# Opening reordered around the first x load, and expert pairs normalised two pairs ahead

## The chip, the cores and the metric

The kernel runs on one NeuronCore of a Trainium2 chip. The metric is the device time of one execution in microseconds (us). The median of several executions is compared; a profiled execution has a time of its own.

## The reference

Input x has 64 sequences of 128 tokens, 256 wide (8192 tokens); ctx has 128 tokens of width 192 for each sequence. Two layers follow each other:

```python
# 1. gated cross attention, 16 heads of 16
q = layernorm(x) @ wq + bq;  k = ctx @ wk + bk;  v = ctx @ wv + bv
out = softmax(q @ k.T / 4) @ v
x = x + tanh(g_xattn) * (out @ wo + bo)
# 2. gated switch layer: 32 experts of hidden width 64, one expert for each token
h = layernorm(x)
e = argmax(h @ router_w.T + router_b)
y = relu(relu(h @ w1[e] + b1[e]) @ w2[e] + b2[e])
x = x + tanh(g_ffn) * y
```

## The kernel before, in words

Each engine has a program of its own, written out in full, and they meet only by semaphores: SP issues DMAs, POOL (GpSimd), ACT (ScalarE), DVE (VectorE) and PE (TensorE) work in the order of their program and stop at the first wait that is not met. Matrix products keep float32 accuracy by splitting each operand into a float16 "hi" part (a cast on ACT) and a "lo" part (a subtraction on DVE or POOL).

The attention stage works on 16 groups of 4 sequences (512 tokens). `schedule(step)` calls `step` for s = -4 to 17. Within step s, group s+4 (`nxt`) gets its statistics on DVE (`x_stats`, `stats_2`) and is normalised by POOL into `xn`; group s+3 (`a`) gets queries, keys and values; group s+1 (`n1`) gets score maxima; group s (`g`) gets exponentials, the product with v and the output projection; group s-1 (`f`) the second layer norm and logits; group s-2 (`r`) its place among its expert's rows, and is scattered to `expert_rows`. So steps -4 to -1 only fill the pipe, and few of their parts lie beside other work. SP loads x of group s+4 into the one buffer `xin` when POOL has normalised the group before (`xn_done`), writes q and k to `q_image` and `k_image`, and reads them back in another layout (`qstk`, `kstk`). It also loads the raw weights of two experts at each step (`w1r`, `w2r`) behind the last key part (`k_lo`); ACT waits for them at the end of its step (L647), scales and casts them, and POOL makes the lo parts one step later.

Ahead of step -4 stands the preparation of the shared weights. SP issues wq and wk, then x and ctx of group 0, the gate, ten small or medium loads and a few constants. ACT waits for the gate (tanh, L593), scales and casts wq, wk, the biases, the router weights, widens bv (`bvb`), scales and casts wv. PE multiplies bv with wo (L1043), ACT makes wo from it, and DVE makes all lo parts. Only behind the last of these does DVE's first `x_stats` stand.

After the last group the tokens lie sorted by expert. The expert stage takes 96 tiles of 128 rows, two by two: 48 pairs. `tiles_schedule(fstep, lead)` calls `fstep` for p = -lead to 50, and `at_(d)` is pair p+d. For pair j: DVE and ACT normalise one tile each (`normed`, L1001 and L731) into `gn`, which has two buffers; PE transposes (`moved`, L1304); ACT casts (`moved_hi`, L739) and DVE subtracts (`moved_lo`, L1007); PE multiplies with w1 (`hidden`, L1314 and L1317); ACT and DVE make hi and lo of the hidden layer (`hidden_hi` L745, `hidden_lo` L1013); PE multiplies with w2 (`output`, L1328 to L1330); ACT applies relu (`relu_out`, L752); DVE adds the residual (`finish`, L1022 and L1024, semaphore `f_out`); POOL scatters the two tiles to `out` (L572). SP reloads a tile's buffer, of which there are 16, behind `f_out` (L426). The matmuls take the expert's columns by an address in a register.

The orders within one `fstep` are: PE moved(0), hidden(-1), output(-2); ACT normed(+1), moved_hi(0), hidden_hi(-1), relu_out(-2); DVE normed(+1), moved_lo(0), hidden_lo(-1), finish(-2).

Of the kernel before, what the change touches and what calls it, by code (L numbers as in the profile page):

```python
# [99 lines left out]
def build(nc, x, ctx_t, g2, wq, bq, wk, bk, wv, bv, wo, bo, rw, rb, w1, b1, w2, b2, out):  # L100
    es = ExitStack()
    with es:
# [129 lines left out]
        gn = yin_flat.rearrange("p (a u n) -> p a u n", a=2, u=2)  # L232
# [9 lines left out]
        names = """consts w_in w_in2 w_raw8 w_hi w_lo g_in tanh_done bias_in bv_wide bvwo_ready  # L242
# [67 lines left out]
        def _(sp):  # L310

            sp.dma_start(wraw[:, 0:2, :], wq.rearrange("(t p) n -> p t n", p=P)).then_inc(s_["w_in"], 16)
            sp.dma_start(wraw[:, 2:4, :], wk.rearrange("(t p) n -> p t n", p=P)).then_inc(s_["w_in"], 16)

# [12 lines left out]
            sp.dma_start(gate[:, :], g2.partition_broadcast(P)).then_inc(s_["g_in"], 16)  # L327
            sp.dma_start(bqk[:, 0, :], bq).then_inc(s_["bias_in"], 16)
            sp.dma_start(bqk[:, 1, :], bk).then_inc(s_["bias_in"], 16)
# [6 lines left out]
            sp.dma_start(wraw2[:, 0:2, :], wv.rearrange("(t p) n -> p t n", p=P)).then_inc(s_["w_in2"], 16)  # L336
            sp.dma_start(wraw2[:, 2:4, :], wo.rearrange("(t p) n -> p t n", p=P)).then_inc(s_["w_in2"], 16)
# [17 lines left out]
            def step(s):  # L355
                a, n1, g = s.plus(3), s.plus(1), s
                if s.off > -4:
                    load_x(s.plus(4))
                if a.real():
# [18 lines left out]
                    wait(sp, s_["ew_r8"], a.count(2))  # L378
                    wait(sp, s_["ew_lo"], a.count(2))
                    sp.dma_start(w1r[:, :], w1[:, a.count(SLICE * KT * H):a.count(SLICE * KT * H, SLICE * KT * H)]).then_inc(ew_in, 16)  # L380
                    sp.dma_start(w2r[:, :], w2[:, a.count(SLICE * D):a.count(SLICE * D, SLICE * D)]).then_inc(ew_in, 16)
# [58 lines left out]
        def _(pool):  # L440
# [54 lines left out]
            def step(s):  # L495
                nxt, a, p, g, f, r = s.plus(4), s.plus(3), s.plus(2), s, s.plus(-1), s.plus(-2)
# [17 lines left out]
                if p.real():  # L514

                    wait(pool, s_["ew_hi"], p.count(2, 2))
                    o1, c1 = p.count(SLICE * KT * P), SLICE * KT * P
# [4 lines left out]
                    o2, c2 = p.count(SLICE * D), SLICE * D  # L522
# [60 lines left out]
        def _(act):  # L583
# [8 lines left out]
            act.wait_ge(s_["g_in"], 16)  # L592
            a_.activation(tg[:], gate[:], ACT.Tanh).then_inc(s_["tanh_done"], 1)  # L593
# [6 lines left out]
            act.wait_ge(s_["bias_in"], 16 * 8)  # L600
            a_.activation(bqk8[:], bqk[:], ACT.Copy, scale=WS).then_inc(s_["w_hi"], 1)
            a_.activation(b2raw[:, 0, :], b2raw[:, 0, :], ACT.Copy, scale=WS * WS / 2).then_inc(s_["b2_w"], 1)
            a_.activation(b2raw[:, 1, :], b2raw[:, 1, :], ACT.Copy, scale=WS / 2).then_inc(s_["w_hi"], 1)
            a_.activation(rw_raw[:], rw_raw[:], ACT.Copy, scale=WS).then_inc(s_["w_hi"], 1)
            act.wait_ge(s_["w_hi"], 5)
            act.wait_ge(s_["b2_w"], 1)
            a_.copy(b2hl[:], b2raw).then_inc(s_["b2_hi"], 1)
            a_.copy(rw_s[:, 0, :, :], rw_raw[:]).then_inc(s_["b2_hi"], 1)
            a_.copy(bvb[:], bvc[:].unsqueeze(2).to_broadcast([P, KT, P])).then_inc(s_["bv_wide"], 1)
            act.wait_ge(s_["w_in2"], 32)  # L610
# [4 lines left out]
            act.wait_ge(s_["bvwo_ready"], 1)  # L615
            act.wait_ge(s_["tanh_done"], 1)
            a_.activation(wraw2[:, 2:4, :], wraw2[:, 2:4, :], ACT.Copy, scale=WS).then_inc(s_["w_raw8"], 1)
            act.wait_ge(s_["w_raw8"], 7)
            a_.activation(wraw2[:, 2:4, :], wraw2[:, 2:4, :], ACT.Identity, scale=tg[:, 0:1]).then_inc(s_["w_raw8"], 1)
            act.wait_ge(s_["w_raw8"], 8)  # L620
            a_.copy(wo_s[:, 0, :, :], wraw2[:, 2:4, :]).then_inc(s_["w_hi"], 1)
# [57 lines left out]
            def step(s):  # L679
                a, n1, g, f = s.plus(3), s.plus(1), s, s.plus(-1)  # L680
# [33 lines left out]
                if a.real():  # L714

                    expert_raw(a)
                    expert_hi(a)
# [9 lines left out]
            def normed(p):  # L727
                j, i, m, lap = p
                act.wait_ge(t_in[(2 * j + 1) % NT], (2 * j + 1) // NT * 16 + 16)
                wait(act, s_["f_t"], j + (-1))  # L730
                a_.activation(gn[:, i, 1, :], gt[lap % 2][:, 2 * m + 1, 0:D], ACT.Identity,  # L731
                              bias=gt[lap % 2][:, 2 * m + 1, D + 1:D + 2], scale=gt[lap % 2][:, 2 * m + 1, D:D + 1]
                              ).then_inc(s_["f_norm1"], 1)
# [28 lines left out]
            tiles_schedule(fstep, lead=1)  # L762
# [3 lines left out]
        def _(dve):  # L766
            v_ = nc.vector

            def carry(site):

                v_.tensor_copy(carry_v[:, site:site + 1], tg[:, 0:1])
# [4 lines left out]
            dve.wait_ge(s_["w_hi"], 2)  # L776
            v_.tensor_tensor(wq_s[:, 1, :, :], wraw[:, 0:2, :], wq_s[:, 0, :, :], ALU.subtract).then_inc(s_["w_lo"], 1)
            v_.tensor_tensor(wk_s[:, 1, :, :], wraw[:, 2:4, :], wk_s[:, 0, :, :], ALU.subtract).then_inc(s_["w_lo"], 1)
            dve.wait_ge(s_["b2_hi"], 2)
            for n in (E, 3 * E):  # L780
                v_.tensor_tensor(b2hl[n:n + E, :, :], b2raw[n:n + E, :, :], b2hl[n:n + E, :, :], ALU.subtract).then_inc(s_["b2_lo"], 1)
            v_.tensor_tensor(rw_s[:, 1, :, :], rw_raw[:], rw_s[:, 0, :, :], ALU.subtract).then_inc(s_["w_lo"], 1)

            dve.wait_ge(s_["w_hi"], 6)
            v_.tensor_tensor(wv_s[:, 1, :, :], wraw2[:, 0:2, :], wv_s[:, 0, :, :], ALU.subtract).then_inc(s_["w_lo"], 1)

            dve.wait_ge(s_["bvwo_ready"], 1)
            v_.tensor_tensor(gbias[:], AV[0][:, 0:D], bo_b[:], ALU.add).then_inc(s_["gb_a"], 1)
            dve.wait_ge(s_["gb_a"], 1)
            dve.wait_ge(s_["tanh_done"], 1)  # L790
            v_.tensor_scalar(gbias[:], gbias[:], tg[:, 0:1], None, ALU.mult).then_inc(s_["gb_done"], 1)
            dve.wait_ge(s_["w_hi"], 7)
            v_.tensor_tensor(wo_s[:, 1, :, :], wraw2[:, 2:4, :], wo_s[:, 0, :, :], ALU.subtract).then_inc(s_["w_lo"], 1)
            dve.wait_ge(s_["pool_set"], 1)
            v_.tensor_tensor(etmp[:, 0:2, :], ident[:, 0:2 * E].rearrange("p (a e) -> p a e", e=E),
                             ident[:, 2 * E:4 * E].rearrange("p (a e) -> p a e", e=E), ALU.add).then_inc(s_["b2_lo"], 1)
# [597 lines left out]
```

## Time and profile before

| | |
|---|---|
| median of 3 executions | 835.28 us (832.35 to 839.61) |
| the profiled execution's own time | 844.19 us |
| its span, first to last instruction | 842.4 us, so 1.8 us lie around it |
| PE, DVE, ACT, POOL busy | 76%, 64%, 50%, 54% |
| opening: PE's first score exponentials | at about 90 us |
| attention steps | about 90 to 600 us |
| sorting, expert tables and first tiles | about 600 to 645 us |
| expert pairs | 645 to 834 us |

An engine's row in the trace tells when an instruction began and how long it took; in brackets behind it stands how long the engine had been idle and what ended that. In the chain of waits each piece is followed back from the end to what released it. "remote" and "another core or an unknown queue" mean that the semaphore came at a time at which no recorded instruction ended. Ends of matmuls are modelled.

### The profile page before, as it was taken

Reading aid. Unit: us, or ns where it says so; the run is one execution under the profiler, and the core shown is the slowest. Engines: PE = TensorE matmul, PEld = TensorE weight load, DVE = VectorE, ACT = ScalarE, POOL = GpSimd, SP = SyncE. Lnnn points to the kernel's source line nnn. Section 1 sums busy time; section 2 is a strip of 40 time slices with the busy share of each in tenths; the row PEclk is TensorE's granted clock in tenths of the full one; section 3 lists DMA queues with packets and bytes.
Section 4 is the critical chain, followed back from the end, with each engine's and each line's share of the span. In section 5 each row is a group of like instructions: output and inputs, shape, how many; then the busy total and the mean of one; then the engine's idle time right before and its main releaser. Section 6 shows DMA issues by size and latency. Waiting matters only on the chain.

```text
span 842.4 us, 21593 instructions
## 1 busy us (share of the span) xinstructions
PE 643.5 (76%) x7526; PEld 412.2 (49%) x7526; DVE 537.5 (64%) x1338; ACT 420.6 (50%) x805; POOL 455.3 (54%) x690
## 2 busy tenths in 40 slices
PE   0557889988988989889889889779406777777772
PEld 0223455555555565565555555455305655545551
DVE  3236578877878778779769777563534555564652
ACT  4232666755755666566557466335104545344441
POOL 3453655677676775675675745145322554555554
PEclk9977799999999999999999996885756888988886
DMA  4398764774674664765755553101065443433310
GB/s 129 117 201 180 185 147 144 189 184 129 166 178 132 170 152 153 182 140 166 172 148 161 129 138 65 47 28 51 13 201 172 132 129 111 123 112 121 114 46 0
DMA packets 77863, 110.71 MB, mean 131 GB/s; under 512 B 11398, under 2 KB 64443, under 8 KB 74688
## 3 DMA queue, kind: packets, MB, share of 16 engines
q1 hardware_dynamic: 67776, 90.28, 42.7%
q0 software_dynamic: 7680, 16.93, 5.7%
q10 hardware_dynamic: 2304, 2.13, 0.8%
q8 instruction: 64, 1.05, 0.5%
q14 instruction: 39, 0.32, 0.1%
HBM read 70.90 MB, written 42.27 MB: 134 GB/s over the span
## 4 chain that ended last, share of the span: by engine, by line
PE 54%; DVE 18%; another core or an unknown queue 6%; issue 6%; ACT 6%; DMA 3%; SPq 3%; POOL 2%; ACTq 0%; DVEq 0%; POOLq 0%
PE M L1178 10%; PE AV L1101 8%; PE S L1079 7%; PE M L1267 6%; PE ST L1317 5%; DVE mx L814 5%; PE AV L1206 3%; DVE xt L843 3%; PE ST L1178 3%; DVE ot L921 2%; PE S L1206 2%; PE S L1250 2%; PE M L1153 2%; DMA w2r<-w 2%
## 5 line engine op out<-in xcount | busy, mean ns | idle before, releaser
L814 DVE TENSOR_REDUCE mx<-S 128x4 f32<-128x512 f32 x256 | 170.9, 685 | 27.4 <-PE S L1079 25.6
L627 ACT ACTIVATE pt<-ST 128x512 f32<-128x512 f32 x256 | 150.5, 603 | 44.3 <-PE ST L1085 43.6
L1079 PE MATMUL S<-kstk,qstk 48*128 48x128 f16 x1024 | 103.4, 224 | 16.2 <-DVE mx L814 14.1
L1101 PE MATMUL AV<-pt,v 128*18 128x128 f32 x2048 | 108.3, 292 | 5.3 <-ACT pt L627 3.8
L1085 PE MATMUL ST<-qstk,kstk 49*128 49x128 f16 x1024 | 105.5, 227 | 0.5 <-ACT pt L627 0.5
L1079 PEld LDWEIGHTS S<-kstk,qstk 48*128 48x128 f16 x1024 | 59.1, 96 | 81.2 <-issue 47.6
L445 POOL TENSOR_TENSOR carry_p<-zero_e 128x1 f32<-128x1 f32 x97 | 19.8, 204 | 138.0 <-DVE posn L1024 75.4
L551 POOL DMA_INDIRECT expert_rows<-x,posi x64 | 63.3, 989 | 17.2 <-issue 17.2
L1304 PE MATMUL S<-ident,yin 128*128 128x128 f32 x192 | 37.5, 328 | 43.7 <-DVE yin L1001 38.4
L1317 PE MATMUL ST<-qs,w1s 128*128 128x128 f16 x576 | 68.2, 249 | 0.9 <-issue 0.5
L1085 PEld LDWEIGHTS ST<-qstk,kstk 49*128 49x128 f16 x1024 | 59.8, 97 | 5.2 <-issue 4.3
L1267 PE MATMUL M<-wo_s,xt 128*128 128x256 f16 x384 | 52.7, 302 | 9.7 <-DVE xt L843 9.7
L843 DVE TENSOR_TENSOR xt<-M,xt 128x512 f16<-128x512 f32 x64 | 43.4, 679 | 25.7 <-ACT xt L660 17.5
L1178 PE MATMUL M<-xt,wq_s 128*128 128x512 f16 x192 | 52.6, 418 | 7.5 <-DVE xt L843 7.5
L572 POOL DMA_INDIRECT out<-xn,posn x48 | 47.9, 997 | 15.8 <-issue 15.8
L572 POOL DMA_INDIRECT out<-xin,posn x48 | 47.3, 985 | 16.7 <-issue 16.7
L752 ACT ACTIVATE xn<-AV 128x512 f32<-128x512 f32 x48 | 28.8, 601 | 50.5 <-remote 42.7
L705 ACT CAST xt<-S 128x512 f16<-128x512 f32 x32 | 17.6, 588 | 72.3 <-PE S L1250 72.3
L1101 PEld LDWEIGHTS AV<-pt,v 128*18 128x18 f32 x2048 | 36.5, 98 | 35.2 <-issue 7.3
L529 POOL TENSOR_TENSOR ids<-ids,group_c 128x4 int32<-128x4 int32 x16 | 3.2, 197 | 93.3 <-DVE mv L807 93.3
L1304 PEld LDWEIGHTS S<-ident,yin 128*128 128x128 f32 x192 | 25.2, 165 | 54.6 <-DVE yin L1001 44.3
L1267 PEld LDWEIGHTS M<-wo_s,xt 128*128 128x128 f16 x384 | 40.5, 108 | 22.2 <-issue 13.7
(192 smaller groups left out, 1523.0 us busy)
## 6 DMA issues: line engine op xcount, KB each, us to landing
xin<-x SPq DMA_DIRECT2D x16, 512.0 KB, 6.1
yin<-ctx_t SPq DMA_DIRECT2D x16, 512.0 KB, 6.9
q_image<-qs SPq DMA_DIRECT2D x64, 128.0 KB
k_image<-ks SPq DMA_DIRECT2D x64, 128.0 KB
qstk<-q_image SPq DMA_DIRECT2D x32, 256.0 KB, 5.1
kstk<-k_image SPq DMA_DIRECT2D x32, 256.0 KB, 7.4
xres<-x SPq DMA_DIRECT2D x16, 512.0 KB, 4.5
x<-expert_rows SPq DMA_DIRECT2D x48, 130.0 KB
```

Of the source, the lines that this page charges most:

```text
L551: g_.indirect_dma_start(out=rows[:, :], out_offset=bass.IndirectOffsetOnAxis(ap=posi[:, b:b + 1], axis=0), in_=x2[:, r.par, b, :], in_offs ...
L572: g_.indirect_dma_start(out=out, out_offset=bass.IndirectOffsetOnAxis(ap=ido[:, m:m + 1], axis=0), in_=yo[m // 2][:, m % 2, :], in_offset= ...
L627: a_.activation(pt[:, c % NPT, :], ST[c % 2][:], ACT.Exp, scale=0.25 / (WS * WS)).then_inc(s_["exp_done"], 1)
L814: v_.reduce_max(mx[:, b, CH * cc:CH * cc + CH], S[(c + 1) % 2][:].rearrange("p (h t) -> p h t", h=CH), X).then_inc(s_["s_max"], 1)
L843: v_.tensor_tensor(dst, src, hi, ALU.subtract).then_inc(s_[done], 1)
L1079: last = t_.matmul(S[(c + 1) % 2][:, cols], qstk[row:row + STACK, n1.tri, hp, tok], kstk[row:row + STACK, n1.tri, hp, tok], start=True, st ...
L1085: last = t_.matmul(ST[c % 2][:, cols], kstk[row:row + STACK + 1, g.tri, hp, tok], qstk[row:row + STACK + 1, g.tri, hp, tok], start=True, s ...
L1101: last = t_.matmul(AV[b % 2][32 * i:32 * i + VW, cc * P:(cc + 1) * P], v[:, g.tri, h:h + VW], pt[:, c % NPT, i * P:(i + 1) * P], start=Tru ...
L1178: last = t_.matmul(bank, w, m, start=(n == 0), stop=(n == len(pairs) - 1))
L1267: last = t_.matmul(M[b // 2][:, (b % 2) * D:(b % 2) * D + D], at[:, i, t, tok], wo_s[:, j, t, :], start=(t == 0 and n == 0 and b % 2 == 0) ...
L1304: last = t_.transpose(S[i][:, col:col + P], gn[:, i, u, k * P:(k + 1) * P], ident[:])
L1317: last = t_.matmul(bank, w1s[:, w, bass.ds(e + k * P, P)], gx[:, i, x_, u, k, :], start=False, stop=(n == KT * 3 - 1))
```

## The change

The opening: SP issues x and ctx of group 0 first, then the two biases of q and k, then wv, then the rest with wo last. The loads of wq, wk and the gate go to ACT's queue. On DVE the statistics of group 0 stand first, then only the lo parts of wq, wk and wv. Everything else of the shared weights (tanh, bv with wo, router weights, expert biases, wo) moves behind step -3's own work on ACT, PE and DVE (`late_weights`). In steps -3 and -2 DVE makes the statistics of the next group between the query and the key lo parts (c == 7), no longer at the end of the step. The raw expert weights are loaded, cast and split one step later than before: SP and ACT for group s+2, POOL for group s+1.

The expert stage: `gn` gets a second pair of buffers (in `xres`), pairs are normalised two ahead, the normalisation stands third in each engine's step, and `finish` comes one step later, d = -3.

In the diff, cut to its core, `late_weights` and the expert casts are ACT's first and DVE's after that; the two wait lines of `normed` are alike on ACT and DVE.

```diff
-            sp.dma_start(wraw[:, 0:2, :], wq.rearrange("(t p) n -> p t n", p=P)).then_inc(s_["w_in"], 16)
-            sp.dma_start(wraw[:, 2:4, :], wk.rearrange("(t p) n -> p t n", p=P)).then_inc(s_["w_in"], 16)
...
             load_x(Group(0))
-            sp.dma_start(gate[:, :], g2.partition_broadcast(P)).then_inc(s_["g_in"], 16)
...
+            act.dma_start(wraw[:, 0:2, :], wq.rearrange("(t p) n -> p t n", p=P)).then_inc(s_["w_in"], 16)
+            act.dma_start(wraw[:, 2:4, :], wk.rearrange("(t p) n -> p t n", p=P)).then_inc(s_["w_in"], 16)
+            act.dma_start(gate[:, :], g2.partition_broadcast(P)).then_inc(s_["g_in"], 16)
             act.wait_ge(s_["w_in"], 32)
...
-                if a.real():
-                    expert_raw(a)
-                    expert_hi(a)
+                if s.off == -3:
+                    late_weights()
+                if p.real():
+                    expert_raw(p)
+                    expert_hi(p)
...
+                    if nxt.real() and a.real() and not n1.real() and c == 7:
+                        next_stats(nxt)
...
-                if nxt.real():
...
+                if nxt.real() and n1.real():
+                    next_stats(nxt)
+                if s.off == -4:
+                    next_stats(nxt)
+                    early_weights()
+                if s.off == -3:
+                    late_weights()
...
-                wait(act, s_["f_t"], j + (-1))
+                wait(act, s_["f_t"], j + (-3))
...
-                for d, stage in ((1, normed), (0, moved_hi), (-1, hidden_hi), (-2, relu_out)):
+                for d, stage in ((0, moved_hi), (-1, hidden_hi), (2, normed), (-2, relu_out)):
...
-                for d, stage in ((1, normed), (0, moved_lo), (-1, hidden_lo), (-2, finish)):
+                for d, stage in ((0, moved_lo), (-1, hidden_lo), (2, normed), (-3, finish)):
...
-            tiles_schedule(fstep, lead=1)
+            tiles_schedule(fstep, lead=2)
```

`carry`, a tiny instruction of DVE ahead of each aggregation, becomes a memset instead of a copy, since `tg` is not there yet.

## Rows read from the trace of the kernel before

**Rows 1.** Busy time by stage: the opening, and the expert stage; PEclk is the granted clock.

```profile
core 0: us, PE busy (x) PEld busy (x) DVE busy (x) ACT busy (x) POOL busy (x), PEclk, DMA share, GB/s
0.00:25.00 25.00, 2.05 (x4) 1.20 (x5) 8.02 (x22) 8.99 (x21) 10.94 (x43) 1.00 0.36 109
663.20:810.50 147.30, 112.48 (x863) 79.38 (x861) 81.87 (x180) 66.64 (x144) 78.64 (x108) 0.86 0.39 114
```

**Rows 2.** The chain of waits: start us, us, what.

```profile
2.88 5.83 DMA gate<-g
...
13.40 2.06 PE AV L1043 x4
...
17.55 0.69 DVE wo_s L793
...
18.60 1.32 DVE st L801 x4
...
25.00 1.96 PE M L1125 x8
...
39.15 6.61 DMA w2r<-w
...
60.14 6.30 DMA w2r<-w
...
535.11 4.13 PE M L1267 x24
```

**Rows 3.** Instructions in order of time, 0 to 55 us.

```profile
0.81 1.28 ACT L593 ACT_TABLE_LOAD   x1 [0.81 <-PEq L1388]
...
7.24 0.28 POOL L479 TENSOR_SCALAR_AFFINE_SELECT ident<-ident 128x128 f32<-128x128 f32 x1
...
20.54 0.20 POOL L486 TENSOR_TENSOR ve<-mv,eps_c 128x4 f32<-128x4 f32 x1 [13.02 <-DVE mv L807]
...
34.02 0.75 DVE L845 SCALAR_TENSOR_TENSOR qs<-M,bqk,qs 128x512 f16<-128x512 f32 x1 [1.42 <-ACT qs L665]
...
38.30 0.60 ACT L712 ACTIVATE v<-ST 128x512 f32<-128x512 f32 x1 [0.49 <-PE ST L1178]
...
47.80 1.06 ACT L660 CAST xt<-M 128x512 f16<-128x512 f32 x2
...
54.97 0.75 DVE L845 SCALAR_TENSOR_TENSOR qs<-M,bqk,qs 128x512 f16<-128x512 f32 x1 [0.96 <-ACT qs L665]
```

**Rows 4.** DMA issues, windows 0:24, 24:38 and 38:57; last: us to landing.

```profile
xin<-x SPq DMA_DIRECT2D x1, 512.0 KB, 5.3
...
xin<-x SPq DMA_DIRECT2D x1, 512.0 KB, 3.6
...
xin<-x SPq DMA_DIRECT2D x1, 512.0 KB, 11.5
```

**Rows 5.** Instructions in order of time, two pairs of the expert stage.

```profile
704.14 0.60 ACT L752 ACTIVATE xn<-AV 128x512 f32<-128x512 f32 x1 [2.56 <-remote]
...
704.77 0.75 DVE L1022 SCALAR_TENSOR_TENSOR xn<-xn,tg,v 128x512 f32<-128x512 f32 x1 [2.74 <-ACT xn L752]
...
705.51 0.41 DVE L1001 TENSOR_SCALAR yin<-x 128x256 f32<-128x256 f32 x1
...
705.95 0.69 DVE L1007 TENSOR_TENSOR qs<-S,qs 128x512 f16<-128x512 f32 x1
...
705.97 1.11 PE L1304 MATMUL S<-ident,yin 128*128 128x128 f32 x4 [1.54 <-DVE yin L1001]
...
706.88 0.31 PE L1314 MATMUL ST<-pick,b2hl 128*128 x1
...
712.25 0.60 ACT L752 ACTIVATE xn<-AV 128x512 f32<-128x512 f32 x1 [1.83 <-remote]
```

**Rows 6.** Who waited for whom, 665 to 820 us: total, times, longest.

```profile
ACT xn L752 <- remote: 40.8, 17, 3.3
```

**Rows 7.** ACT's relu of two pairs near the start of the expert stage.

```profile
651.60 0.60 ACT L752 ACTIVATE xn<-AV 128x512 f32<-128x512 f32 x1 [0.90 <-PE AV L1330]
...
657.71 0.60 ACT L752 ACTIVATE xn<-AV 128x512 f32<-128x512 f32 x1 [0.36 <-PE AV L1330]
```

More of the change, by code:

```diff
@@ L355, in step @@
             def step(s):
-                a, n1, g = s.plus(3), s.plus(1), s
+                a, p, n1, g = s.plus(3), s.plus(2), s.plus(1), s
                 if s.off > -4:
@@ L376, in step @@
                                      ).then_inc(k_out, 16)
[L378 to L381, printed above, removed]
+                if p.real():
+                    wait(sp, s_["ew_r8"], p.count(2))
+                    wait(sp, s_["ew_lo"], p.count(2))
+                    sp.dma_start(w1r[:, :], w1[:, p.count(SLICE * KT * H):p.count(SLICE * KT * H, SLICE * KT * H)]).then_inc(ew_in, 16)
+                    sp.dma_start(w2r[:, :], w2[:, p.count(SLICE * D):p.count(SLICE * D, SLICE * D)]).then_inc(ew_in, 16)
                 send_max(n1)
@@ L599, in _ @@
             a_.copy(wk_s[:, 0, :, :], wraw[:, 2:4, :]).then_inc(s_["w_hi"], 1)
-            act.wait_ge(s_["bias_in"], 16 * 8)
+            act.wait_ge(s_["bqk_in"], 32)
             a_.activation(bqk8[:], bqk[:], ACT.Copy, scale=WS).then_inc(s_["w_hi"], 1)
[L602 to L610, printed above, removed]
+            act.wait_ge(s_["w_hi"], 3)
+            act.wait_ge(s_["w_in2"], 16)
             scaled(wraw2[:, 0:2, :])
@@ L679, in step @@
             def step(s):
-                a, n1, g, f = s.plus(3), s.plus(1), s, s.plus(-1)
+                a, p, n1, g, f = s.plus(3), s.plus(2), s.plus(1), s, s.plus(-1)
                 for c in range(CHUNKS):
@@ L779, in _ @@
[L779 to L796, printed above, removed]
@@ L807, in stats_2, with next_stats @@
                     v_.bn_aggr(mv[:, b, :], st[:, b, :]).then_inc(s_[mv_sem], 1)
+            def next_stats(nxt):
+                dve.wait_ge(x_in[nxt.par], nxt.halved(16, 16))
+                wait(dve, s_["xn_done"], nxt.count(1))
+                for b in range(GB):
+                    x_stats(b)
+                stats_2(st1, mv1, "ln1_st", "ln1_mv", nxt, 0)
             def max_chunk(n1, c):
@@ L1030, in fstep @@
                         stage(p)
-            tiles_schedule(fstep, lead=1)
+            tiles_schedule(fstep, lead=2)
         @block.tensor
@@ L1037, in _, with late_weights @@
             t_ = nc.tensor
-            pe.wait_ge(s_["av_set"], 1)
-            pe.wait_ge(s_["bv_wide"], 1)
-            pe.wait_ge(s_["w_in2"], 32)
-            for t in range(KT):
-                last = t_.matmul(AV[0][:, 0:D], bvb[:, t, :], wraw2[:, 2 + t, :], start=(t == 0), stop=(t == KT - 1))
-            last.then_inc(s_["bvwo_ready"], 1)
-            pe.wait_ge(s_["pool_set"], 1)
-            pe.wait_ge(s_["w_lo"], 5)
+            pe.wait_ge(s_["pool_set"], 1)
+            pe.wait_ge(s_["w_lo"], 3)
+            def late_weights():
+                pe.wait_ge(s_["av_set"], 1)
+                pe.wait_ge(s_["bv_wide"], 1)
+                pe.wait_ge(s_["w_in3"], 16)
+                for t in range(KT):
+                    last = t_.matmul(AV[0][:, 0:D], bvb[:, t, :], wraw2[:, 2 + t, :], start=(t == 0), stop=(t == KT - 1))
+                last.then_inc(s_["bvwo_ready"], 1)
             def scores_wait(n1, c):
@@ L1225, in step @@
                     values(1)
+                if s.off == -2:
+                    pe.wait_ge(s_["w_lo"], 5)
+                    pe.wait_ge(s_["gb_a"], 1)
                 if n1.real():
@@ L1253, in step @@
                     values(3)
+                if s.off == -3:
+                    late_weights()
                 if g.real():
```

95 lines of the change are left out of this document (60 added, 35 removed).

## The prediction

> **What bounds the kernel now.** I read three views in this order. Busy time by stage first: in the first 25 us PE is busy for 2.05 us, and in the expert stage, the other place that the change touches, PE is busy for 112.5 of 147.3 us and no other engine for more than 82 [rows 1]. So the opening is a chain of latencies, and in the expert stage everybody waits part of the time. The chain of waits then names them. It goes through the gate's DMA, ACT's casts, the bv-wo product, wo's lo part at 17.55, and only then reaches the statistics of x at 18.60 and the first transposes at 25.00 [rows 2]. Later it stands twice on the raw expert weights, 6.61 and 6.30 us, with ACT's cast of the next group's xt queued behind the wait. Last, instructions in order of time for two expert pairs [rows 5]: relu at 704.14, finish at 704.77, normalisation at 705.51, transposes at 705.97, hidden product at 706.88, next such relu at 712.25. The reader should see that PE idled 1.54 us for a normalisation that stood behind finish on DVE, and that had waited for nothing else. Such late relus come 17 times in 155 us (two more have PE named), about every 8.1 us, that is every two pairs [rows 5, 6]. Their semaphore comes at a time at which no recorded matmul ended: PE reports in clumps.
>
> The attention steps from 90 to 600 us keep their order on every queue. I cost them at nothing: SP, ACT and POOL still carry one load, one cast and one split of expert weights per step, at the same place in each program, for a group one lower. The extra ones fall at step 13. ACT's 2.1 us (w1r at 45.8 to xt at 47.8, behind the landing in rows 2 and 3) then lie beside PE's output projection, which took 4.13 us at 535.11 [rows 2]; uncovered they would cost 2.1 once. The memset for the copy saves or costs under 0.1 us a step off the path.
>
> **The opening, start.** Removed from the path: gate, all weights but x. x is issued at about 0.8. The same 512 KB landed 5.3 us after issue behind wq and wk, and 3.6 alone [rows 4]. Sharing with the loads that ACT now issues I take 5.3, so 6.1. Statistics took 1.94 (18.60 to 20.54), and from there to the transposes 4.46 (to 25.00) [rows 2, 3]. POOL is free at 7.52 [rows 3], under 8.04. So PE starts at 12.5 in place of 25.0: gain 12.5. If x takes 3.6, POOL's constants set 7.52 and the gain is 13.0. PE also waits for three lo parts of weights; ACT now issues three DMAs and the table load (1.28) first [rows 3], which lies under the landing, and casts from about 7 on. I expect the wv part before 12; if it comes at 15, the gain is 10.
> What the DMA queues do is seen in rows 4 only as 5.3 against 3.6. The Trainium skill (DMA: Bandwidth & Descriptors, Issuing engines are not separate DMA queues) says that loads issued from ACT and SP share the same engines and interleave, so x would not overtake wq and wk for free; this agrees with taking 5.3, and costs 0.5 us against the row of 3.6.
>
> **The opening, step -3.** Its statistics for group 1 now stand behind the second query lo part, which ended 9.8 us after PE's start (34.77 less 25.00) [rows 2, 3]. x of group 1 is issued as POOL ends, lands 3.6 later, and is there. They hold the key lo parts by up to 1.94, about 0.6 of it behind PE's own pace. Group 1 reaches PE at 9.8 + 1.94 + 4.46 = 16.2. ACT drops the wait of 6.61 and its casts, and takes the late weights after its last v at 38.90, which is 13.9 after PE's start. Queued there: tanh and bv, two small instructions taken as 0.25 each, PE's product 2.06, ACT's wo, 2.1 (15.5 to 17.55) [rows 2]. They end at 18.6; then ACT casts xt, which before began 22.8 after PE's start (47.80) [rows 3]. DVE's wo lo part (0.69) ends at 19.3, about when it is wanted. Gain 4.1. If a second table load comes for tanh, 1.28 of that is lost [rows 3].
>
> **The opening, step -2.** The wait for raw weights (6.30) stays, since the first expert load is now here, and its issue stands behind the key lo parts. In front of these now stand the statistics of group 2: 0.6 as above. x of group 2 took 11.5 us to land, behind the q and k images [rows 4], issued at 44.7. In the new order it is issued some 20.3 after PE's start and wanted by DVE at 26.6: before, the second query lo part ended 7.9 after the xt cast (55.72 less 47.80), and that cast now stands at 18.7 [rows 3]. With 11.5 DVE stalls 5.2 us; with 3.6 not at all. The two raw expert loads are no longer ahead of it; I take the middle, 2.5. Loss 3.1, between 0.6 and 5.8. What is queued behind DVE's wait: both key lo parts, so SP's k image and the expert load, so ACT's next xt.
> Opening together: 12.5 + 4.1 - 3.1 = 13.5, between 8 and 17.
>
> **The expert stage.** The edit takes the ring relu, finish, normalisation, transposes out. Two pairs walked through from a late relu at time 0 (704.14) [rows 5]: transposes of the next pair are not held, their normalisation was done a step before. ACT: relu, 0.49 later moved_hi (its normalisation stood there before), ended at 1.06. DVE: moved_lo at once, since finish of that pair now comes a step later, 0.69, ended at 1.77; PE's hidden product 0.24 later (as 706.64 to 706.88), at 2.01. Before it was 2.74. So 0.73 of each clump goes, if PE's reports come as late after its restart as before (5.4 us, from 706.88 to 712.25). What is late next is moved_hi behind relu. 17 + 2 clumps [rows 6] make 13.9.
> Costs: at the start ACT and DVE stop for the fifth pair's tiles a step earlier, with relu of the first pair behind it: about 0.5. At the end finish is a step later with one more standing in front (0.75 and a copy [rows 5]), and POOL's scatters follow: between 0 and one pair at 3.05 us, taken as 2. The reload of a tile buffer starts a step later and is wanted one earlier, three steps of about 4 us apart, far above a load. New wait: relu of j needs finish of j-2, now behind hidden_lo of j. Finish and copy (0.75, 0.16) end before PE has made output j. Together 13.9 - 2.5 = 11.4. Below: 0 less 2.5; above, the next rival.
>
> **Sum.** 13.5 + 11.4 = 24.9. The profiled execution's 844.19 becomes 819.3. It lies 8.9 over the median; taking the difference off the median gives 810.4. I forecast 810.
>
> **Rivals.** (A) The clumps dissolve. Near the stage's start two pairs took 6.11 us (651.60 to 657.71) with PE named as releaser each time [rows 7], against 8.11. If the lead lets PE stay there, 19 clumps give 38: 835.3 - 13.5 - 38 + 2.5 = 786. For it speaks that nothing but PE was waited for there; against, that the late reports began with no change in the program. Half of it gives 797 or so.
> (B) The clump's rhythm is PE's reporting, and time taken from one wait appears in the next. Two pairs took about 8.1 with the clock low in part or high (0.86 on average [rows 1]). Then the expert stage costs 2.5: 824.
> (C) Slower: the new ring bites. If reports still come in clumps, the second relu of a clump must wait for a finish that now stands behind hidden_lo and a normalisation on DVE. Price per clump: normalisation, finish and copy, 0.41 + 0.75 + 0.16 = 1.3 plus PE's restart 0.24, 1.5, with none of the 0.73 gained. 19 of them cost 29; 835.3 - 13.5 + 29 + 2.5 = 853. It decides against the opening from 0.6 us a clump on. In the walk above that finish is done four steps of an engine earlier, so I give it little.
> (D) The opening gives only its lower bound, DVE stalling on x and the weights late: 8 in place of 13.5: 816.
> A rule that would change this: cheap functions now come before tanh on ACT. In the trace there is one table load, 1.28 us, ahead of tanh [rows 3]. The Trainium skill (ScalarE: Activation LUTs, Table sets: the hidden batching unit) has functions such as copy in every set; a first load for them may name another set than tanh's, and it prices a switch at about 2.7 us. By that the opening gives 10.8; it lies inside D.
>
> **How the numbers follow.** Forecast 0.42, A or most of it 0.18, B 0.2, C 0.04, D 0.16. A measurement of this kernel tells about 1% (8.4 us) from no change. Faster by over 1% is below 826.9: the forecast, A, D and nearly all of B: 0.93. Within 1%: B with a poor opening, 0.04. Slower 0.03. The range leaves out C and the far half of A: 795 to 826.
>
> **What would show it.** The first transposes near 12.5 us; no wait of ACT on the raw weights before step -2, one there of about 6 us; DVE's third statistics with an idle time before them of 0 to 5 us, ended by x's DMA. PE's transposes in the expert stage never released by DVE's L1001; time between late relus about 7.4 in place of 8.1.  Wrong would be: late relus still 8.1 apart (B), or gone (A), or relu released by DVE's L1024 (C).

## The result, and the profile after

| | before | after |
|---|---|---|
| median of runs | 835.74 us (832.35 to 839.61, 4 runs) | 812.13 us (806.66 to 819.44, 4 runs) |
| the profiled execution's own time | 844.19 us | 806.66 us |
| its span | 842.4 us | 804.9 us |

The medians are 23.6 us apart. The ratio is 0.9694, with a 95% interval of 0.9623 to 0.9766, which makes 25.6 us. (A ratio leaves out executions in the slower of the chip's two states, here the 819.44; a median doesn't, so gains in us are worked out from ratios below.) Beside two later series of before, each on one chip, the same kernel stood at 0.9754 (0.9702 to 0.9806) and 0.979 (0.9753 to 0.9827), 20.7 and 17.7 us less. So 20 us is the better figure, and the two profiled executions, 37.5 us apart, exaggerate it.

Busy time by stage of the kernel after, the opening and the expert stage, answering to [rows 1]:

```profile
core 0: us, PE busy (x) PEld busy (x) DVE busy (x) ACT busy (x) POOL busy (x), PEclk, DMA share, GB/s
0.00:25.00 25.00, 9.61 (x38) 4.88 (x39) 9.54 (x28) 9.04 (x17) 16.62 (x47) 1.00 0.54 165
643.00:788.60 145.60, 112.58 (x955) 85.34 (x952) 92.44 (x202) 74.10 (x158) 91.85 (x122) 0.90 0.39 118
```

PE works 9.6 us of the first 25 in place of 2.05. In the second stretch PE runs 955 matmuls in 145.6 us, where it ran 863 in 147.3, at nearly the same busy time: the clock is higher (0.90 for 0.86) and the other engines, DVE and POOL above all, stand still less.

The chain of waits after, 0 to 60 us, answering to [rows 2]:

```profile
3.53 2.88 POOL v L469
...
7.27 0.27 POOL ident L477
...
9.78 3.59 POOL xn L558 x4
13.50 1.95 PE M L1148 x8
...
29.15 1.63 DVE b2hl L795
30.81 1.42 DVE b2hl L795
32.26 1.07 DVE etmp L796
33.46 1.18 DVE rw_s L800
...
37.23 4.75 PE M L1201 x12
...
43.39 1.40 DVE st L811 x4
...
47.88 6.97 DMA w2r<-w
```

Gate, bv-wo product and wo are gone from the path ahead of PE's first transposes, which begin at 13.50 in place of 25.00. Ahead of the normalisation the path now runs through POOL's own constants, which end at 7.54, and not through x. The raw expert weights are waited for once, 6.97, not twice. New on the path is a block on DVE from 29.15 to 35.97 in step -3, late weights, in which the two b2hl parts and etmp take 1.5 and 1.1 where they took 0.7 and 0.2 at their old place.

The same stretches in order of time, answering to [rows 3]:

```profile
2.42 1.28 ACT L587 ACT_TABLE_LOAD   x1 [2.42 <-issue]
...
5.39 1.41 DVE L811 BATCH_NORM_STATS2 st<-xin 128x6 f32<-128x256 f32 x4 [3.38 <-DMA xin<-x]
...
9.76 3.59 POOL L558 TENSOR_SCALAR xn<-xin,rs,ve 128x256 f32<-128x256 f32 x4
...
10.18 0.69 DVE L786 TENSOR_TENSOR wq_s<-xn,wq_s 128x512 f16<-128x512 f32 x1 [2.96 <-ACT wk_s L598]
...
27.07 0.19 ACT L609 ACTIVATE tg<-gate 128x2 f32<-128x2 f32 x1
...
29.15 3.08 DVE L795 TENSOR_TENSOR b2hl<-ot,b2hl 32x512 f16<-32x512 f32 x2 [3.08 <-ACT rw_s L618]
...
30.19 1.49 POOL L502 TENSOR_TENSOR ys<-yin,zero_e 128x512 f16<-128x512 f32 x1
```

One table load, at 2.42, and none before tanh at 27.07. POOL's normalisation of x (L558) takes 3.59 while DVE's lo parts of wq, wk and wv run beside it; at step -3, where no such work stood beside it, the same instructions took 2.18. In step -3 the two b2hl parts take 3.08 beside POOL's L501 to L504.

Who waited for whom in the expert stage after, 643 to 789 us: total, times, longest. It answers to [rows 6]:

```profile
ACT ks L752 <- remote: 24.1, 9, 3.9
...
PE ST L1342 <- DVE qs L1027: 14.1, 11, 1.9
...
ACT xn L759 <- remote: 8.3, 9, 2.2
...
PE S L1332 <- DVE yin L1021: 0.9, 1, 0.9
```

The late relus are down from 40.8 us in 17 waits to 8.3 in 9, but the same kind of wait, a semaphore of PE that comes where no recorded matmul ended, now shows at ACT's cast of the hidden layer (L752), for 24.1 us. That cast was held before too: it waited 40.0 us then, with PE's hidden product named, and the 24.1 stand beside 16.1 of that kind now. PE waited for DVE's normalisation once.

### The profile page after: what moved, and what is told of

It reads as the page before. It is cut to its first block, busy times and chain, and to the rows that moved or that the text cites. A ratio compares the mean times of both kernels' runs of the same rounds, so it can differ in the third digit from the quotient of the medians.

```text
span 804.9 us, 21592 instructions
## 1 busy us (share of the span) xinstructions
PE 616.0 (77%) x7526; PEld 402.8 (50%) x7526; DVE 541.9 (67%) x1338; ACT 420.0 (52%) x805; POOL 461.8 (57%) x690
## 4 chain that ended last, share of the span: by engine, by line
PE 54%; DVE 20%; issue 8%; ACT 7%; another core or an unknown queue 4%; POOL 3%; SPq 2%; DMA 2%; POOLq 0%; ACTq 0%; DVEq 0%
PE M L1201 11%; PE AV L1124 7%; PE M L1295 7%; PE S L1102 6%; DVE mx L832 6%; PE ST L1201 4%; PE AV L1229 3%; DVE xt L861 3%; PE ST L1345 3%; DVE ot L941 2%; PE S L1276 2%; PE S L1229 2%; DVE st L903 2%; DVE qs L1027 1%
## 5 line engine op out<-in xcount | busy, mean ns | idle before, releaser
L1102 PE MATMUL S<-kstk,qstk 48*128 48x128 f16 x1024 | 100.7, 220 | 22.7 <-DVE mx L832 20.3
L1124 PE MATMUL AV<-pt,v 128*18 128x128 f32 x2048 | 102.8, 278 | 5.5 <-ACT pt L632 4.4
L1108 PE MATMUL ST<-qstk,kstk 49*128 49x128 f16 x1024 | 100.4, 219 | 0.5 <-ACT pt L632 0.5
L1345 PE MATMUL ST<-qs,w1s 128*128 128x128 f16 x576 | 64.7, 243 | 1.1 <-issue 0.8
L570 POOL DMA_INDIRECT out<-xin,posn x48 | 50.6, 1055 | 16.5 <-issue 16.2
L1108 PEld LDWEIGHTS ST<-qstk,kstk 49*128 49x128 f16 x1024 | 56.9, 94 | 3.4 <-issue 1.7
L710 ACT CAST xt<-S 128x512 f16<-128x512 f32 x32 | 17.6, 588 | 75.1 <-PE S L1276 75.0
L570 POOL DMA_INDIRECT out<-xn,posn x48 | 48.2, 1004 | 14.1 <-issue 14.1
L861 DVE TENSOR_TENSOR xt<-M,xt 128x512 f16<-128x512 f32 x64 | 43.4, 679 | 14.2 <-ACT xt L665 9.3
L1295 PEld LDWEIGHTS M<-wo_s,xt 128*128 128x128 f16 x384 | 40.8, 108 | 22.7 <-issue 14.0
L752 ACT ACTIVATE ks<-ST 128x256 f16<-128x256 f32 x48 | 18.7, 390 | 58.9 <-remote 26.5
L1345 PEld LDWEIGHTS ST<-qs,w1s 128*128 x576 | 44.2, 106 | 9.8 <-issue 2.0
L1033 DVE SCALAR_TENSOR_TENSOR ks<-ST,ks 64x256 f16<-64x256 f32 x48 | 20.5, 428 | 42.2 <-ACT ks L752 23.2
```

The source lines that it names most:

```text
L570: g_.indirect_dma_start(out=out, out_offset=bass.IndirectOffsetOnAxis(ap=ido[:, m:m + 1], axis=0), in_=yo[m // 2][:, m % 2, :], in_offset= ...
L861: v_.tensor_tensor(dst, src, hi, ALU.subtract).then_inc(s_[done], 1)
L1102: last = t_.matmul(S[(c + 1) % 2][:, cols], qstk[row:row + STACK, n1.tri, hp, tok], kstk[row:row + STACK, n1.tri, hp, tok], start=True, st ...
L1108: last = t_.matmul(ST[c % 2][:, cols], kstk[row:row + STACK + 1, g.tri, hp, tok], qstk[row:row + STACK + 1, g.tri, hp, tok], start=True, s ...
L1124: last = t_.matmul(AV[b % 2][32 * i:32 * i + VW, cc * P:(cc + 1) * P], v[:, g.tri, h:h + VW], pt[:, c % NPT, i * P:(i + 1) * P], start=Tru ...
L1295: last = t_.matmul(M[b // 2][:, (b % 2) * D:(b % 2) * D + D], at[:, i, t, tok], wo_s[:, j, t, :], start=(t == 0 and n == 0 and b % 2 == 0) ...
```

## The experiments

The first four kernels shared one chip (before: 842.52 us median, 17 runs), the next four another (752.64, 23 runs), the last four a third (840.88, 11 runs). Ratios are to before on the same chip.

**The two halves.** e1_open is the changed kernel with the expert stage of before; e2_expert the reverse: the opening of before with the expert stage of the change.

```diff
 e1_open, against after (e2_expert: the opposite lines, against before)
-                for d, stage in ((0, moved_lo), (-1, hidden_lo), (2, normed), (-3, finish)):
+                for d, stage in ((1, normed), (0, moved_lo), (-1, hidden_lo), (-2, finish)):
...
-            tiles_schedule(fstep, lead=2)
+            tiles_schedule(fstep, lead=1)
```

Expected of the changed kernel again, beside them:

> The changed kernel once more, on the same chip as its parts, to have the four against one another. Expected 23 to 25 us under the kernel before (ratio about 0.97), and from its second profile whether the attention steps between the opening and the sorting really are 7 us shorter (as between the first two profiles) or whether that was the granted clock of one execution: if the latter, the 13 steps between the second and the fifteenth group's first maximum take again within 2 us of the 418.6 of before, in one of the two profiles of the kernel before or here.

Of the opening alone:

> The opening of the changed kernel with the expert stage of before. If the trace of the change is read rightly, its gain is 9 to 12 us (11.5 at the first transposes, 1 in step -3, less 1 in step -2), not the 13.5 of the prediction: 825 us. If the gains of the two parts do not add (expert stage depending on where it begins), it differs from this by more than 4 us.

Of the expert stage alone:

> The opening of before with the expert stage of the changed kernel. By the trace pairs 5 to 45 gain 20 us, the first pairs lose 2.6 and the end loses 2: 15 us less than before, 820 us. The prediction's walk gave 11.4. The rival that the rhythm is PE's own and nothing is gained gives 835 to 838.

Measured: a0_after 824.24 us, 0.9754 (0.9702 to 0.9806). e1_open 825.04 us, 0.9787 (0.9751 to 0.9824). e2_expert 836.65 us, 0.9946 (0.991 to 0.9981). So the opening is worth 17.9 us (14.8 to 21.0) and the expert stage 4.5 (1.6 to 7.6); together 22.4, and a0_after has 20.7 (16.3 to 25.1), so the two add within the noise. Two of my expectations missed: the opening gave more than the 9 to 12 us that I read from its trace, and the expert stage far less than the 15. The 836.65 of e2_expert lies where I had put the rival that nothing is gained, but that figure went by a before of 835; beside the 842.52 of this chip a small gain is left.

**Late weights one step later.** In step -3 DVE and POOL are both busy. e3_late2 moves `late_weights` to step -2, and PE's waits for them to step -1.

```diff
-                if s.off == -3:
+                if s.off == -2:
                     late_weights()
...
-                if s.off == -2:
+                if s.off == -1:
                     pe.wait_ge(s_["w_lo"], 5)
```

> The changed kernel with the late weights another step later (step -2), on ACT in front of the wait for the raw expert weights. In the profile of the change DVE's late block took 6.7 us of step -3, with instructions of 0.7 us taking 1.1 to 1.6 beside POOL's, and held xt of group 1. Theory: out of step -3 it frees 4 to 5 us there and is hidden in step -2 by the DMA wait of 7 us: 4 us under the changed kernel. Rival: in step -2 DVE's part ends after the wait and the gain is given back there: within 1 us of the changed kernel.

Measured: 822.97 us, 0.977 (0.9723 to 0.9818); nothing to tell from a0_after, as the rival had it. Its instructions in order of time say why:

```profile
43.87 1.41 DVE L811 BATCH_NORM_STATS2 st<-xin 128x6 f32<-128x256 f32 x4 [5.98 <-DMA xin<-x]
...
47.02 1.40 DVE L795 TENSOR_TENSOR b2hl<-ot,b2hl 32x512 f16<-32x512 f32 x2
48.45 0.23 DVE L796 TENSOR_TENSOR etmp<-ident 128x64 f32<-128x64 f32 x1
...
48.82 0.22 DVE L800 TENSOR_TENSOR rw_s<-ot,rw_s 128x64 f16<-128x64 f32 x1
```

The late block on DVE now takes 3.5 us (47.02 to 50.57) in place of 6.8, and what stands behind it in step -3 comes 5 us earlier (both xt lo parts are made at 32.2, not 37.2). But x of group 2 can't land earlier: it is issued at 33.55 (33.19 in after) and takes 10.3 us, and DVE stalls 5.98 on it. What the better place gave, that landing took. The block isn't without a neighbour here either: it lies beside POOL's small instructions and its normalisation of x (L558, 48.73 to 51.52), and it is these that pay, 2.79 for L558 in place of 2.18.

**The clumps on another chip, and PE's addresses.** On this chip I wanted to see whether addresses from registers make PE report late. e6_fixed is before, and e7_fixed_new after, with the expert of a tile fixed at build time, so that the output of their second layer is another. b1_before is the kernel before itself. e4_finish_early is after with `finish` at its old step, for the question which of the two edits of the expert stage counts.

```diff
 e6_fixed and e7_fixed_new
-                    one[t] = pe.snap((words[t // PACK] >> (5 * (t % PACK))) & (E - 1))
-                    held[t] = pe.snap(one[t] * D)
+                    one[t] = t % E
+                    held[t] = one[t] * D
 e4_finish_early (and e9_lead2_alone), against after
-                for d, stage in ((0, moved_lo), (-1, hidden_lo), (2, normed), (-3, finish)):
+                for d, stage in ((0, moved_lo), (-1, hidden_lo), (2, normed), (-2, finish)):
```

> The kernel before once more, for a second profile of it. The attention steps took 418.6 us with the clock low for 37.5 us of them in its first profile, and 411.7 with 17.1 low in the first profile of the change, 415.3 with 30.7 low in the two parts. If that is the clock's phase in one execution and not the change, this one lies on the same line: 418.6 less 0.34 us for each microsecond less of low clock. If the change did it, this one is near 418.6 whatever the clock.

> The changed kernel with finish again two steps behind (d = -2), the rest of the change kept. The walk of the prediction took 0.73 us out of each clump partly because finish no longer stood behind a late relu in front of the next lo part; with finish at -2, that lo part waits for finish (0.75 us) again, the clump is as long as before, and pairs 5 to 45 take 158 to 162 us in the profile (before 161.7, changed 141.5 and 156.1): 4 to 8 us slower than the changed kernel in the times, with 2 us given back at the end. Rival: the lead alone does it, and finish later only costs its tail of 2 us: 2 us faster than the changed kernel.

> The kernel before, with tile t of the expert stage multiplied by the weights of expert t mod 32 at an address fixed in the program, not by those of its own expert at an address from a register. The output of the second layer is therefore another. Theory: PE's late reports (relu released at a time at which no recorded matmul ended) come from matmuls whose address is worked out by its sequencer; with fixed addresses the 17 remote waits are gone and two pairs take about 6.1 us as at the start of the stage, pairs 5 to 45 about 125 us in place of 161.7: 35 us faster. Rival: they come from the matmuls themselves or from what surrounds them: two pairs still take about 8.1 us, within 5 us of before.

> The same in the changed kernel: tile t by expert t mod 32 at a fixed address. If PE's reports are then in time, the ring that the change takes out (relu, finish, normalisation, transposes) is no longer what is waited for, and this is no faster in the expert stage than the kernel before with fixed addresses, only by the opening: 12 to 17 us under it in all. If the lead is worth something by itself, 5 us more.

Measured: b1_before 752.52 us (0.9995), e4_finish_early 738.29, 0.98 (0.9776 to 0.9824), e6_fixed 752.24, 0.9994 (0.9976 to 1.0011), e7_fixed_new 742.61, 0.9868 (0.9846 to 0.989). e4_finish_early had no run of the changed kernel beside it on this chip, so its own question stays open here; e7_fixed_new is 9.6 us under e6_fixed by medians, less than the 12 to 17 that I expected. The surprise is b1_before. The same program is 90 us faster here, and has no clumps. Of the 87.7 us between its profile and the first one, 33.9 lie in the attention steps and 46.5 in the 40 expert pairs. Its busy time in the 40 pairs from the fifth relu on, and who waited for whom from 620 to 738 us:

```profile
618.08:733.34 115.26, 103.50 (x962) 78.53 (x961) 91.17 (x202) 78.89 (x160) 90.11 (x122) 1.00 0.52 156
```

```profile
ACT xn L752 <- PE AV L1330: 12.4, 40, 0.4
```

Every relu waits for the matmul that makes its input, 0.3 us on average, and a pair takes 2.88 us; nothing is "remote". The same 40 pairs of before in the first profile, at a granted clock of 0.86:

```profile
657.71:819.43 161.72, 124.35 (x959) 88.39 (x958) 90.08 (x200) 74.25 (x160) 86.72 (x120) 0.86 0.37 110
```

So the late reports don't come from the program alone, but with the chip on which it runs, and what fixed addresses do to them can't be judged where there are none.

What fixed addresses do here is seen in the traces, though not in the total. The 40 pairs of e6_fixed:

```profile
612.32:720.05 107.73, 91.07 (x960) 69.83 (x960) 89.56 (x197) 78.57 (x160) 89.61 (x115) 0.98 0.57 168
```

PE is busy for 91.1 us in place of 103.5 and the pairs take 7.5 less, but what comes behind them takes 28.7 in place of 21.4. The chain of waits tells why: over the pairs 33% of it is PE's hidden product (L1317) in b1_before, and 37% POOL's scatter (L572) in e6_fixed. With PE faster the scatters bind, and the gain ends as a queue of scatters. The same holds for e7_fixed_new, which loses 4 us to e4_finish_early: its chain runs through the scatters too, its pairs take 109.5 for 113.3, and what follows 29.0 for 21.3. It has `finish` a step later as well, but e6_fixed, which hasn't, shows the same 7 us behind the pairs.

The attention steps, which b1_before was to judge, take 384.7 us here at a granted clock of 0.98. That is far under my line from the clock (405.8 with no low clock left), so the clock doesn't explain the two chips; but 383.3 in e4_finish_early and 384.1 in e7_fixed_new, beside 384.7 and 383.9 in the two with the old opening, say that the change costs nothing there.

**Lead and finish apart, where there are clumps.** a1_after is the changed kernel again, e9_lead2_alone the same text as e4_finish_early, and e5_finish_alone keeps the lead of one and the old order, with `finish` a step later:

```diff
 e5_finish_alone, against before's loops (its opening is the new one)
-                for d, stage in ((1, normed), (0, moved_lo), (-1, hidden_lo), (-2, finish)):
+                for d, stage in ((1, normed), (0, moved_lo), (-1, hidden_lo), (-3, finish)):
```

> The changed kernel once more, beside the three that follow. On a chip like the second one (before at 752) my count is: opening 16 us, expert stage 0 to 2 us, so a ratio of 0.979 +- 0.003, as with the finish one step earlier. On a chip like the first two (before at 835 to 845): 0.972 to 0.976.

> The changed kernel with finish at its old step (two pairs behind), lead of two kept. If the lead carries the expert stage's gain: as the changed kernel, or up to 2 us faster, because the end of the stage is a pair step shorter (end after the last hidden product 14.7 in place of 16 to 18 us). If the later finish carries it: slower than the changed kernel by 5 to 10 us on a chip that shows the late relus, no difference on one that doesn't.

> The new opening and the finish one step later, normalisation with the old lead of one pair. My walk through a clump has the old normalisation behind finish; with finish a step later the normalisation on DVE stands behind moved_lo and hidden_lo alone, so about the same 0.7 us of a clump should go: as the changed kernel within 3 us. If only the longer lead frees PE, it stands with the opening alone, 4 to 6 us above the changed kernel on a chip with late relus.

Measured: a1_after 823.96 us, 0.979 (0.9753 to 0.9827). e9_lead2_alone 827.68, 0.9846 (0.98 to 0.9892). e5_finish_alone 825.65, 0.9816 (0.9777 to 0.9856). By the times the intervals overlap, so they don't tell them apart; and as the opening alone wasn't run on this chip, they don't say either what is left for the expert stage here. The traces tell more. Starts of relus (L759) of e9_lead2_alone, in order of time:

```profile
688.05 0.60 ACT L759 ACTIVATE xn<-AV 128x512 f32<-128x512 f32 x1 [2.78 <-remote]
689.78 0.61 ACT L759 ACTIVATE xn<-AV 128x512 f32<-128x512 f32 x1
696.21 0.60 ACT L759 ACTIVATE xn<-AV 128x512 f32<-128x512 f32 x1 [2.88 <-PE AV L1358]
697.94 0.61 ACT L759 ACTIVATE xn<-AV 128x512 f32<-128x512 f32 x1
704.33 0.60 ACT L759 ACTIVATE xn<-AV 128x512 f32<-128x512 f32 x1 [2.84 <-remote]
```

688.05 to 696.21 to 704.33: the period of 8.1 us for two pairs, as in [rows 5]. And those of the kernel after:

```profile
649.49 0.60 ACT L759 ACTIVATE xn<-AV 128x512 f32<-128x512 f32 x1
...
654.87 0.60 ACT L759 ACTIVATE xn<-AV 128x512 f32<-128x512 f32 x1
...
656.60 0.61 ACT L759 ACTIVATE xn<-AV 128x512 f32<-128x512 f32 x1
```

The rhythm is lost: 5.38, then 1.73. I counted, among the 39 pairs from the fifth on, for how many the relu two pairs further begins 8.03 to 8.27 us later, and put the stage together from starts of relus and of PE's first transposes (us; a0_after was profiled in its longest execution, 829.06):

| kernel | in the 8.1 rhythm | first transposes to 5th relu | 40 pairs | next 3 | to the end of the span |
|---|---|---|---|---|---|
| before | 34 | 25.0 | 161.7 | 8.3 | 14.7 |
| e1_open | 30 | 24.5 | 160.4 | 7.8 | 15.0 |
| e9_lead2_alone | 26 | 30.2 | 155.9 | 8.1 | 14.7 |
| e5_finish_alone | 9 | 25.6 | 156.2 | 8.7 | 16.5 |
| after | 0 | 27.6 | 141.5 | 10.3 | 16.3 |
| a0_after | 2 | 25.3 | 156.1 | 7.9 | 18.7 |
| a1_after | 2 | 26.0 | 153.7 | 9.0 | 17.8 |
| e2_expert | 2 | 26.0 | 152.9 | 9.0 | 17.8 |
| e3_late2 | 0 | 25.4 | 152.5 | 8.8 | 16.1 |
| e10_apart | 2 | 26.0 | 155.7 | 7.2 | 18.1 |

With the lead alone the lock on 8.1 us largely stays; with the later `finish` alone it is mostly broken, and with both it is gone. Each alone shows 5 us less in the 40 pairs, both together 9.0 (mean of six, 152.1, against 161.05), at the price of 2.6 at the end, 1.3 at the start and 0.7 in the three pairs after. The 9.0 leans on the first profile: without its 141.5 the mean is 154.2 and the gain 6.9, and two of the six (156.1 and 155.7) are no better than either edit alone.

**DVE and POOL.** e10_apart holds DVE's three early lo parts until POOL has normalised x.

```diff
             def early_weights():
+                dve.wait_ge(s_["xn_done"], 1)
```

> The changed kernel, where DVE starts its lo parts of wq, wk and wv only after POOL's normalisation of x of the first group has ended. Contention theory: POOL's normalisation takes about 2.2 us again in place of 3.59, and each lo part of DVE keeps the 0.70 that it takes alone; PE's first transposes, which need both, then come within 1 us of the changed kernel's, since what POOL gains DVE loses by starting later. Rival (POOL's 3.59 is due to DMA traffic of the loads): it stays at about 3.6. Total time: same within 1 us by both.

Measured: 824.9 us, 0.9798 (0.9756 to 0.9841). In order of time:

```profile
10.04 2.16 POOL L558 TENSOR_SCALAR xn<-xin,rs,ve 128x256 f32<-128x256 f32 x4
...
12.23 1.52 DVE L787 TENSOR_TENSOR wq_s<-xn,wq_s 128x512 f16<-128x512 f32 x1 [4.50 <-POOL xn L558]
13.17 1.48 POOL L502 TENSOR_TENSOR ys<-yin,zero_e 128x512 f16<-128x512 f32 x1
...
16.86 1.94 PE L1149 MATMUL M<-ident,xn 128*128 128x128 f32 x8 [16.86 <-DVE wv_s L790]
```

POOL's normalisation is back at 2.16 from 3.59, with the loads as before: its extra time is DVE's doing, not DMA traffic's. The other half of my expectation was wrong. DVE's parts then fell beside POOL's next instructions and took 1.52 to 1.64 each in place of 0.69, POOL's L502 1.48 in place of 1.04, and PE began at 16.86, 3.4 later than after, not within 1. Group 2's first row maximum comes at 113.8 in place of 110.9 (a1_after); the total can't show 3 us.

## Why the prediction came out right, and which of its terms did not

The forecast was 24.9 us less, 810; measured were 812.1 and 23.6 less by the medians (25.6 by the ratio), and 20.7 and 17.7 in the repeats. The total came out right partly by luck: two of its terms were wrong in opposite directions, 13.5 for the opening and 11.4 for the expert stage, against 17.9 and 4.5 with each part alone, and the repeats have less than the first series.

**The opening, start.** Gain 11.5 for 12.5. x came 0.7 earlier than I took (statistics at 5.39, their normal 1.41 long), so that POOL's constants, which end at 7.54, set its start, as in my case of 3.6 us; that gave 0.4. ACT's casts began at 7.65, as expected, and the wv part ended at 12.4, for 12, ahead of need. What I missed is that DVE's three lo parts, moved into the gap after the statistics, lie beside POOL's normalisation, which I had taken at its time alone inside the 4.46: 3.59 in place of 2.2, shown by e10_apart. The Trainium skill (SBUF — State Buffer, Who interferes with whom) has the rule that I should have weighed: a DVE instruction with two SBUF inputs contends with a GpSimd instruction that reads SBUF, and who issues first decides who waits. The runs agree that the two contend: in the start POOL alone pays, beside L502 DVE pays as well, and DVE's subtract with one input in PSUM (xt, L861) keeps 0.70 at 16.09, beside POOL's L504 of 15.44 to 16.60. That the order of issue decides it, no run here shows.

**Step -3.** This is the term of the opening that failed most: gain 4.1 expected, 1.0 found. From PE's first transposes to this step's product it took 24.8 us before (25.00 to 49.76) and 23.7 after (13.50 to 37.23). ACT's side was right: no wait for raw weights in this step, its wo cast ended at 31.06, 17.6 after PE's start, where I had 18.6. But I had DVE's wo part end at 19.3 after PE's start, by durations of [rows 2]; it ended at 35.97, 22.5 after. The missing 3.2 is the contention again: the block takes 6.8 beside POOL's instructions with two SBUF inputs (L501 to L510), and 3.5 beside its small instructions and L558 (e3_late2).

**Step -2.** Loss 3.1 expected, 0.9 found: 21.3 us from product to product before (49.76 to 71.04), 22.2 after (37.23 to 59.44). My 2.5 for DVE's stall on x of group 2 did not appear, since step -3 was late itself; x took 9.5 from its issue at 33.19 and the statistics stood without idle time before them. It appears as 5.98 as soon as step -3 is made shorter (e3_late2), close to my upper end of 5.2. So the two errors hang together: x of group 2 landed at 42.7 in after and at 43.9 in e3_late2, and had DVE been on time in step -3, it would have gained 0.7 us at the statistics (43.39) and no more.

To the first row maximum of group 2 the opening gives 12.2 us in the first pair of profiles (121.44 to 109.26; 109.0 in a0_after, 108.4 in e1_open) and 10 to 17 on the faster chip (125.7 and, in e6_fixed with the same opening, 120.6, to 109.0 and 110.4), against 13.5. The 17.9 that e1_open has in timed runs lies at the top of my range of 8 to 17 and is more than its trace shows there (13.0). Its profile is 18.7 us shorter than that of before: 3.4 of the rest lie in the attention steps, 2.3 behind them. Whether the opening causes these isn't shown, so some 5 us of its gain stay open. Only the opening's lower bound (D) was a rival of this part, and it is refuted; so is the rule on a second table load, which I had put inside it: there is one load.

**The attention steps.** Taken at nothing. The two profiles differ there by 6.9 us (418.6 and 411.7), and in the clock. Busy time with the granted clock, before, then after:

```profile
121.44:540.04 418.60, 369.74 (x5122) 231.07 (x5120) 324.45 (x823) 252.05 (x470) 258.80 (x386) 0.96 0.58 149
```

```profile
109.26:520.94 411.68, 362.16 (x5122) 228.25 (x5120) 323.92 (x824) 253.96 (x474) 261.34 (x388) 0.98 0.59 153
```

At 0.96 after takes 418.2 (a0_after) and 415.3 (a1_after), and e2_expert, with the old opening, 415.4. What moves with the clock is PE's busy time, 369.7 against 362.2, while DVE's stays. So on one chip the difference goes with the clock, and the raw weights a step later cost nothing that shows.

**The expert stage.** 13.9 expected for 19 clumps; 9.0 in the 40 pairs (6.9 without the first profile). The ring relu, finish, normalisation, transposes was rightly read. Who waited for whom in e1_open, which has it, 646 to 801 us:

```profile
ACT xn L758 <- remote: 37.0, 16, 2.6
...
PE S L1331 <- DVE yin L1020: 21.0, 19, 2.3
```

Those 21.0 us of PE's become 0.9 in after. But its hidden product waits 14.1 for DVE's moved_lo in place of 3.8, and its output product 6.7 for DVE's hidden lo part in place of 0.3; ACT's wait for the hidden product, 43.1 with all that it names in e1_open, is 50.1, and only the relu's falls, from 41.8 to 15.2. That is rival B's mechanism, time taken from one wait that appears in the next. In five of the six profiles with both edits it holds for all of PE's idle time in the 40 pairs: 37.5 to 39.4 us, against 37.4 in before and 37.6 in e1_open (29.9 in the first profile). What is shorter is PE's busy time, 123 to 124 before and 114 to 117 in these five, at nearly the same clock. The 40 pairs of e1_open, then of a1_after:

```profile
640.53:800.91 160.38, 122.82 (x961) 86.18 (x960) 90.40 (x201) 74.08 (x161) 87.53 (x120) 0.88 0.37 111
```

```profile
644.20:797.91 153.71, 115.42 (x968) 87.29 (x968) 94.17 (x204) 74.82 (x160) 89.02 (x121) 0.89 0.40 119
```

Why the same matmuls keep PE busy for less isn't shown; their ends are modelled. So the step that failed is the one that took 0.73 us of waiting per clump as gained: two pairs take 7.6 us where I had 7.4, against 8.05 before, and not for the reason that I gave. The costs at both ends, 2.5, came out at 4.6: 2.6 at the end for my 2, 1.3 at the start for 0.5, 0.7 between. Together 4.4 by the traces (2.7 without the first profile), 4.5 by the timed runs of e2_expert, for 11.4. B itself (824, a loss of 2.5) is refuted by e2_expert's interval, A (no clumps) by its size, though one of six profiles, the one taken with the result, has 20 us in these pairs; and C by the 8.3 us that relu still waits, none of it put down to `finish`.

Which edit does it: my walk credited the removal of `finish` from in front of moved_lo and of the normalisation from behind `finish` together. The counts give the first more of it (9 pairs in the rhythm against 26). This rests on one profile each, and the times don't confirm it.

**Open.** Why PE's semaphores come late on two chips and not on the third. It isn't that records are missing: the stage has 24 matmuls a pair, and all 1152 are in the trace of before. They come on chips with a lower granted clock in this stage (0.86 to 0.89 against 1.00), but whether the one causes the other isn't shown. In [rows 5] the clock is at the upper level, 2.4 GHz, all through the wait for the late relu at 704.14, and at the lower, 1.2 GHz, behind it:

```profile
701.58:704.14 2.56, 2.01 (x18) 1.20 (x18) 0.43 (x1) 0.00 (x0) 1.37 (x2) 1.00 0.51 159
705.97:709.95 3.98, 3.98 (x24) 2.79 (x24) 2.95 (x6) 1.58 (x4) 2.99 (x4) 0.50 0.48 142
```

So a low clock at that moment isn't needed for a late report.

## What to carry to other kernels

When setup work is moved beside another engine's work, take its duration from a row where that neighbour ran, not from where it ran alone: here the same DVE block was worth 3.5 or 6.8 us by which POOL instructions lay beside it. A step made shorter ahead of a load that is issued from a fixed point gives its gain to that load, so look for the next landing before you move more. And cost each removed wait in a ring with what is late next: of 21 us of PE's waits taken away, 17 came back at its next two products, and each added stage of lead or delay is paid at both ends of the loop.

## What the runs showed of the hardware that I had not expected

- DVE and POOL slow each other where both read SBUF tensors: 0.69 to between 1.52 and 1.64 us for DVE's 128x512 subtract of two SBUF inputs, 2.16 to 3.59 for POOL's normalisation, 1.04 to 1.49 for POOL's addition that casts.
- One program takes 752.5 us on one chip and 840.9 to 842.5 on two others, over 10% apart. A ratio between kernels is worth keeping only from one chip: 18 to 21 us were gained at 841 and 843, and 15 with the earlier `finish` at 753.
- On the slower chips PE's semaphores can come in clumps at times at which no recorded matmul ended, so late that ACT waits up to 5.8 us for one (a0_after; 3.9 in after), and a ring of waits locks to them with a period (8.1 us for two pairs) that the program does not have on the faster chip (5.8).
- With the experts' columns at addresses fixed in the program PE is busy for less than with addresses from a register: 91.1 us in place of 103.5 for 960 matmuls (e6_fixed against b1_before), above all in the hidden product, 36.2 in place of 52.4 for 480. The order of the experts differs as well, so this is one pair of profiles and no clean test; and the total doesn't show it, since POOL's scatters bind then.
